# A gated MLP with adapters and an output projection in fp32 precision: the down projection's ten full blocks in seven block products instead of eight

## What is computed

```
x: (8 sequences, 256 tokens, H = 1024); F = 2752; adapters of rank 16, chosen per sequence
gate = x @ W_gate.T + 0.5 * (x @ A_gate.T) @ B_gate.T
up   = x @ W_up.T   + 0.5 * (x @ A_up.T)   @ B_up.T
act  = silu(gate) * up
x1   = x + act @ W_down.T + 0.5 * (act @ A_down.T) @ B_down.T
out  = x1 + x1 @ weight.T + bias + scale * (x1 @ A.T) @ B.T
```

## Time and profile before

| | us |
|---|---|
| median of three runs | 1662.97 |
| profiled execution, its own time | 1659.71 |
| its span | 1657.6 |
| PE busy | 1620.2 (98%) |
| DVE busy | 1138.4 (69%) |
| POOL busy | 653.5 (39%) |
| ACT busy | 500.8 (30%) |
| granted PE clock, mean | 0.996 |

### The profile page before, as it was taken

One profiled execution on the slowest core, in us unless ns is written; L12 is line 12 of the kernel. 1 busy time (PEld: TensorE's weight loads), 2 busy tenths in 40 slices (PEclk: granted clock), 3 DMA queues, 4 the chain that ended last, 5 costly groups with the idle time before them and its releaser, 6 DMA issues.

```text
span 1657.6 us, 20957 instructions
## 1 busy us (share of the span) xinstructions
PE 1620.2 (98%) x7060; PEld 1315.6 (79%) x7060; DVE 1138.4 (69%) x1302; ACT 500.8 (30%) x833; POOL 653.5 (39%) x441
## 2 busy tenths in 40 slices
PE   6989999999999899999999999999999999999998
PEld 4778888888887788888888788888888887778886
DVE  5987777777769877777777655666655578856433
ACT  3633333333346333333334221111111121431110
POOL 5244444444453444454444443233323331541110
PEclk9999999999999999999999999999999999999999
DMA  8334434433533345334334751122222131013322
GB/s 160 101 80 106 151 98 105 144 84 87 131 90 101 80 108 153 92 105 143 87 85 131 249 148 58 51 79 80 80 53 78 61 70 27 19 29 79 79 50 54
DMA packets 218125, 156.12 MB, mean 94 GB/s; under 512 B 110692, under 2 KB 200164, under 8 KB 215268
## 3 DMA queue, kind: packets, MB, share of 16 engines
q1 hardware_dynamic: 169536, 114.92, 27.4%
q10 hardware_dynamic: 48356, 39.86, 7.6%
q0 software_dynamic: 128, 0.00, 0.0%
HBM read 115.38 MB, written 39.32 MB: 93 GB/s over the span
## 4 chain that ended last, share of the span: by engine, by line
PE 64%; DVE 2%; POOL 1%; issue 1%; DMA 0%; ACT 0%; SPq 0%; DVEq 0%; ACTq 0%
PE ps L1958 64%; DVE tw_down L958 0%; POOL act L1884 0%; POOL Wd L1892 0%; DVE acc L950 0%; DVE X_T L608 0%; DMA raw<-in_x_dram 0%; POOL W L1843 0%; DVE Bd L904 0%; ACT W L1397 0%; DVE Bf L641 0%; DVE tw_down L933 0%; DVE tw_down L931 0%; DVE TU L508 0%; DVE ct L1077 0%
## 5 line engine op out<-in xcount | busy, mean ns | idle before, releaser
L1958 PE MATMUL ps<-X_T,W 128*128 128x512 f32 x1944 | 463.9, 393 | 13.0 <-DVE vbuf L688 5.1
L1958 PE MATMUL ps<-act,Wd 128*128 128x512 f32 x2016 | 462.2, 389 | 1.3 <-POOL Wd L1892 1.3
L1958 PEld LDWEIGHTS ps<-X_T,W 128*128 128x128 f32 x1944 | 365.9, 189 | 97.4 <-DVE vbuf L673 7.4
L1958 PEld LDWEIGHTS ps<-act,Wd 128*128 128x128 f32 x2016 | 378.4, 188 | 81.4 <-POOL Wd L1892 1.7
L1958 PE MATMUL ps<-X_B,W 128*128 128x512 f32 x1728 | 419.0, 392 | 15.3 <-ACT X_B L1426 12.8
L1958 PEld LDWEIGHTS ps<-X_B,W 128*128 128x128 f32 x1728 | 326.4, 189 | 86.6 <-issue 13.2
L950 DVE TENSOR_TENSOR acc<-acc,ps 128x1024 f32<-128x1024 f32 x176 | 214.1, 1219 | 176.5 <-PE ps L1958 175.8
L1843 POOL TENSOR_TENSOR W<-s,W 128x512 fp32r<-128x512 f32 x156 | 211.6, 1357 | 260.4 <-ACT W L1397 260.4
L1843 POOL TENSOR_TENSOR W<-TG,W 128x512 fp32r<-128x512 f32 x88 | 128.4, 1460 | 179.3 <-ACT W L1397 179.3
L1397 ACT ACTIVATE W<-s 128x512 fp32r<-128x512 f32 x156 | 98.4, 632 | 275.5 <-PE ps L1958 264.4
L1884 POOL TENSOR_TENSOR act<-stage,act 128x1024 fp32r<-128x1024 f32 x42 | 100.7, 2415 | 173.4 <-ACT act L1630 173.4
(11 more groups left out here) (135 smaller groups left out, 1522.7 us busy)
## 6 DMA issues: line engine op xcount, KB each, us to landing
stage<-act_scratch SPq DMA_DIRECT2D x21, 1024.0 KB, 5.0
raw<-in_L_cond_W_gate_dram SPq DMA_DIRECT2D x164, 128.0 KB, 3.0
raw<-in_L_cond_W_up_dram SPq DMA_DIRECT2D x164, 128.0 KB, 3.2
raw<-in_x_dram SPq DMA_DIRECT2D x104, 128.0 KB, 3.1
raw<-in_L_cond_W_down_dram SPq DMA_DIRECT2D x88, 128.0 KB, 3.3
act_scratch<-c21buf ACTq DMA_DIRECT2D x42, 256.0 KB, 2.4
act_scratch<-vbuf ACTq DMA_DIRECT2D x42, 256.0 KB, 2.8
xt_scratch<-xt ACTq DMA_DIRECT2D x4, 2048.0 KB, 6.6
```

What stands on the lines that cost most here:

```text
L1958: return nc.tensor.matmul(dst, stationary, moving, start=start, stop=stop, skip_group_check=True)
```

## The change

The full blocks are done in two groups of five. The 2x2 split is over the feature tile (2bb or 2bb+1) and the 512-token column on one side, and over feature tile and even or odd k on the other. In each group seven products (in the order P4, P2, P1, P5, P6, P3, P7) are formed for each token half h: 28 stages. A stage sums over the five blocks, one **step** per block, so there are 140 steps of four 128-row outputs p by THREE, 12 matmuls each. In P2, P1, P3 and P7 a step has two more matmuls, for the adapter. Each p has a bank; bank numbers rotate through seven, and the eighth is the adapter's.

- Phase A makes the sums of `act` that the products need (T1 to T4): four more two-input DVE instructions per two units (`t_first`, `t_second`, `t_fourth`), stored by ACT into `sums_scratch`. vbuf becomes two buffers.
- SP loads one [128, 512] moving operand per step (two in P7) through a ring of four `st`; ACT makes its high part in a ring of four `Tr`, POOL or DVE the low part. `mv_step` says at which step label each engine does it.
- Weights are turned into eight buffers `DW` (two transposes for each item), summed there in place by DVE (`down_sum`), and split into five `Sr`.
- DVE adds each bank to one to four places of `acc`, [128, 512] at a time (`read_bank`), and x from HBM at steps 40 to 87 (`add_residual`).
- `AD_STEP` says at which step label DVE turns the adapter weights of a block. A "label" q is the place in an engine's own order that `down_step(q)` fills.
- The Td and Bd chain stands after all steps.

```diff
+GROUP = 5
+T_RING = 4
+STAGING = 4
...
+        PRODUCTS = ["P4", "P2", "P1", "P5", "P6", "P3", "P7"]
+        B_USES = {"P4": "T4", "P2": "B21", "P1": "B11", "P5": "T1", "P6": "T2", "P3": "B22", "P7": "T3"}
+        B_GIVES = {"P1": ("C11", "C12", "C21", "C22"), "P2": ("C11",), "P3": ("C12",), "P4": ("C21",),
+                   "P5": ("C12", "C22"), "P6": ("C12", "C21", "C22"), "P7": ("C21", "C22")}
+
+        T_OF = {"P2": ("B21", 1, 0), "P1": ("B11", 0, 0), "P3": ("B22", 1, 1), "P7": ("B12", 0, 1)}
+        B_STAGES = [(g, name, h) for g in range(2) for name in PRODUCTS for h in range(2)]
+        STEPS = GROUP * len(B_STAGES)
...
+        def raw_at_step(q):
+
+            items = []
+            if 40 <= q < 88 and q % 3 == 1:
+                items.append(("r", (q - 40) // 24, (q - 40) // 3 % 8))
+            if q in (-1, 0, 1):
+                items += [("D", q + 3, 0), ("D", q + 3, 1)]
+            if 22 <= q < 34 and q % 2 == 0:
+                items.append(("D", 5 + (q - 22) // 4, (q - 22) // 2 % 2))
+            if 61 <= q < 65:
+                items.append(("D", 8 + (q - 61) // 2, (q - 61) % 2))
+            if q in (90, 92):
+                items.append(("D", BLOCKS - 1, (q - 90) // 2))
+            if q in (96, 98):
+                items.append(("Bd", (q - 96) // 2))
+            return items
+
...
+        AD_STEP = {1: 3, 2: 5, 3: 7, 4: 9, 5: 68, 6: 70, 7: 72, 8: 74, 9: 76, 10: 100}
...
+        def mv_step(n):
+
+            return MOVING[n - T_RING][0] + 1 if n >= T_RING else n - 3
+
+        def mv_by_vector(n):
+            q, name, _, h = MOVING[n]
+            return name == "B12" or (h == 1 and name != "T3")
+
...
+        def banks_at_step(q):
+            s, j = divmod(q, GROUP)
+            return s - 1, {0: (0, 1), 1: (2,), 2: (3,)}.get(j, ()) if s > 0 else ()
...
+        def bank_of(s, p):
+            return (4 * s + p) % 7
...
+                    eng.wait_ge(t_stored[1], 16 * (n - 1))
...
+                eng.wait_ge(t_stored[0], 16 * n)
...
+
...
+                V.tensor_tensor(c21buf[:, :], c21buf[:, :], t1buf[:, :], ALU.subtract).then_inc(t_made[3], 1)
...
+            def turn_down(bb, e):
+
+                src = take(("D", bb, e))
...
+                for c in range(2):
+                    last = V.transpose(
+                        DW[bb % len(DW)][:, c, :, e * 64:(e + 1) * 64].rearrange("p k (q i) -> p q k i", q=2),
+                        src[:, :].rearrange("p (q k c i) -> p c q k i", q=2, k=KT, c=2)[:, c])
+                last.then_inc(dw_turned.up((bb, e)), 1)
...
+            def read_bank(s, p):
+
+                eng.wait_ge(pe_s.sem, pe_s.after(("bank", s, p)))
+                for place in places_of(s, p):
+                    h, k, c = place
+                    dst, src = acc[h][:, k, c * TT:(c + 1) * TT], bank_b(bank_of(s, p))
+                    if place in written:
+                        eng.wait_ge(acc_added.sem, acc_added.after(written[place]))
+                        V.tensor_tensor(dst, dst, src, ALU.add).then_inc(acc_added.up((s, p, place)), 1)
+                    else:
+                        V.tensor_copy(dst, src).then_inc(acc_added.up((s, p, place)), 1)
...
+            def down_step(q):
+                s, banks = banks_at_step(q) if q >= 0 else (0, ())
+                for p in banks:
+                    read_bank(s, p)
+                    if p == 0 and s in T_STAGES:
+                        read_t_bank(s)
+                for item in raw_at_step(q):
+                    if item[0] == "r":
+                        add_residual(item)
+                for n in range(len(MOVING)):
+                    if mv_step(n) == q and mv_by_vector(n):
+                        moving_low(n)
+                if 0 <= q < STEPS and B_STAGES[q // GROUP][2] == 0:
+                    g, name, _ = B_STAGES[q // GROUP]
+                    at_ = still_at[g, name, g * GROUP + q % GROUP] + GROUP
+                    if at_ < len(STILL) and STILL[at_] in sw_sum.value:
+                        down_sum(STILL[at_])
+                for item in raw_at_step(q):
+                    if item[0] == "D" and item[1] < BLOCKS - 1:
+                        turn_down(*item[1:])
+                    elif item[0] != "r":
+                        turn_item(item)
+                for bb in range(1, BLOCKS):
+                    if AD_STEP[bb] == q:
+                        turn_ad(bb)
+                if q in (STEPS - 3, STEPS - 2):
+                    last_low(q - STEPS + 3)
...
+            for q in range(-3, STEPS + 3):
+                down_step(q)
+            for pr in range(2):
+                td_first(pr)
+            for p in range(2):
+                bd_low(p)
+            for p in range(2, 4):
+                turn_item(("Bd", p))
...
                 else:
                     sp.wait_ge(ad_turned, bb)
...
+            def load_moving(n):
+
+                _, name, j, h = MOVING[n]
+                if n >= STAGING:
+                    wait_mv_low(sp, n - STAGING)
...
+            def down_step(q):
+                for n, moving in enumerate(MOVING):
+                    if moving[0] == q + 6:
+                        load_moving(n)
+                for item in raw_at_step(q + 4):
+                    if item[0] == "D":
+                        load_down(item)
+                    elif item[0] == "Bd":
+                        load_bd(item)
+                    else:
+                        load_residual(item)
+                for bb in range(1, BLOCKS):
+                    if AD_STEP[bb] == q + 4:
+                        load_ad(bb)
...
+            def moving_high(n):
+                eng.wait_ge(mv_loaded[n % STAGING], 16 * (n // STAGING + 1))
+                if n >= T_RING:
+                    wait_step(eng, MOVING[n - T_RING][0])
+                else:
...
+            def down_step(q):
+                for n in range(len(MOVING)):
+                    if mv_step(n) == q:
+                        moving_high(n)
+                for n in {-3: (0, 1), -1: (2,), 0: (3,), 1: (4,)}.get(q, ()):
+                    still_high(STILL[n])
+                if still_for(q - 1) is not None:
+                    still_high(still_for(q - 1))
+                for bb in range(1, BLOCKS):
+                    if q == (AD_STEP[bb] + 1 if bb < BLOCKS - 1 else STEPS - 3):
+                        ad_high(bb)
...
+                wait_step(eng, STEPS - 1)
...
+            def down_step(q):
+                s, j = divmod(q, GROUP)
+                g, name, h = B_STAGES[s]
+                block_ = g * GROUP + j
+                n = mv_at[q, B_USES[name]]
+                slot, moving = Sr[j], Tr[n % T_RING]
+                eng.wait_ge(sw_lo, still_at[g, name, block_] + 1)
+                wait_mv_low(eng, n)
+                for p in range(4):
+                    if j == 0 and before_in_bank[s, p] is not None:
+                        wait_bank_read(eng, *before_in_bank[s, p])
...
+                    for wl, xl in THREE:
+                        last = matmul(bank_b(bank_of(s, p)), slot[:, wl, p, :], moving[:, xl, :],
+                                      start=(j == 0 and (wl, xl) == (0, 0)),
+                                      stop=(j == GROUP - 1 and (wl, xl) == (1, 0)))
```

734 lines of the change are left out of this document (449 added, 285 removed).

## The result

The changed kernel took **1730.22 us** (median of 4 runs, 1726.67 to 1731.03), against 1662.18 (4 runs): ratio **1.0405, 95% interval 1.0387 to 1.0423**, 68 us slower. I had forecast 1695 with a range of 1648 to 1724. The sign was right, the size was half, and the measured time lies 6 us above the range. The profiled execution took 1731.03 with a span of 1729.3, 71.7 more than the 1657.6 of before; all that follows divides these 71.7 us.

The account below looks back on a forecast made before the run. Phase B was taken as bound by PE's count of matmuls; -54.4 + 8 + 11 + 22 + 19 + 9 + 10.6 + 7 = +32 us on 1659.7 gave 1692, 1695 for the median, range 1648 to 1724.

Parts of the forecast that it names:

- Matmuls: Phase B's full blocks: 1680 matmuls in place of 1920, 240 x 0.227 us saved, -54.4 us.
- A_down's turns, first group: Labels 3 to 9: turns with their loads at least 9.3 us apart, but placed 5.4 apart; +22 us.
- Second group: A_down's turns at labels 68 to 76, with additions of x between: +19 us, at the least 13.
- Start of phase B: Steps 0 to 4: step 0 starts 6.2 us late, later weight items wait for loads; +11, bounds 8 to 14.
- Last block: After the last step PE waits 11.8 us for DVE's chain to Td; +10.6, bounds 8 to 13.
- Phase A: New DVE sums cost 0.8 us each in each half's first units, hidden in ordinary units; +8, bounds 0 to 18.
- ordinary units full: Sign expected in the trace: windows of phase A's ordinary units stay full as before, not beyond 20.06 us.
- DVE over the rest: Other phase B stages: DVE's bank reads and turns overfill some, late by 2.8 and 4.0; +9, bounds 3 to 20.
- 2 for the crowded P7 stages: P7's share of the +9 us for DVE in the rest of phase B: 2 us.
- Rival 3: P7: moving operands late through the ring of four, 20 steps lose 11 us; total 1725, chance 0.17.
- The clock: PE's clock falls after long waits, 1.4 us each, five of some ten holes counted; +7, bounds 2 to 15.
- Where the next wait ends late anyway it costs nothing: Phase B's holes: a lowered PE clock adds no time if the next wait ends late anyway.

Follow-up runs that it names:

- g5: Changed kernel with A_down turns spread, one transpose per A_down block, W_down earlier, activations in pieces, x and Bd work moved, `t_fourth` behind `add_v`: 1668.39 us, ratio 1.0041.
- j1: g5 with the eight DMAs of each A_down block issued four at a time at two labels, and x's additions at other labels: 1653.98 us, ratio 0.9963.
- g3: Changed kernel with PE multiplying zeros while it would wait, at twelve waits of phase B: 1728.46 us, ratio 1.0398.

## Why the prediction was right in sign and wrong in size

- **Matmuls.** Right: 1680, -52.0 for -54.4 us.
- **A_down's turns, first group.** Right in mechanism (turns 9.4 to 12.1 us apart; PE's waits of 2.18, 1.74, 4.80, 5.92 where the walk through the queues had 3.8, 1.3 with 2.6, 5.4 and about 10): 20.3 for 22. **Second group** 24.1 for 19, turns 10.8 to 12.5 apart.
- **Start of phase B.** 14.5 for 11: step 0 starts 6.0 late as computed, the other items of W_down come 3 us later than walked.
- **Last block.** PE waited 10.9 us for Td, forecast 11.8; 12.0 for 10.6.
- **Phase A: mis-sized.** "I take 0.8 each: +8" was 16.6 (12.1 to 16.9 in the ten traces). The ten sums of the first units took 10.9 us, 1.09 each, because four of them began behind a POOL instruction; these units lost 11.4 (16.6 less the next item). The ordinary ones, "hidden" by the prediction, had waits of 5.2: `t_fourth` stood directly ahead of `add_v`, which PE waits for, and the 3 us of DVE's idle time that the prediction counted on lies at another place of the unit. The promised sign "ordinary units full" failed by this much. With `t_fourth` behind `add_v` (g5) two of the nine waits are left. The rule of the Trainium skill (SBUF — State Buffer, "SBUF: two separate sides") says that a DVE instruction with two SBUF inputs and a GpSimd one shut each other out; the trace agrees in every one of the ten sums that met one: a sum that began second ended 0.55 us after the GpSimd instruction, and where that came second it ended 1.15 us after the sum. By that rule alone the prediction had 12.5 for the first units, nearer to their 11.4 than its own 8; over all 80 sums the means are only 0.67 to 0.85 us, as 70 met no GpSimd instruction.
- **"DVE over the rest", the step that failed.** It allowed "2 for the crowded P7 stages", and they lost 16.6. It counted DVE's work and left out SP's queue, where x's, W_down's and A_down's loads stand between the operands: without them P7 is late by 0.4 (g5). Rival 3 named P7, had 11 for it and at 1725 came nearest to the measured time, but its reason (a ring of four operands is short) isn't the cause: in g5 and j1 the same ring runs steps 60 to 69 without waits. Steps 11 to 59 and 80 to 134 lost 9.7 together, where the term had 2.8 and 4.0.
- **Left out, by the same step.** The 1.5 MB of the last block's activations, in the queue ahead of operands: 10.0 us. The prediction priced the last block's chain and not its loads, though it had walked A_down's loads through the same queue.
- **The clock.** Booked at +7 as a term of its own. g3 gives about 1 us for phase B, with its interval of 5: most of it lies inside waits that something else ends. "Where the next wait ends late anyway it costs nothing" was the right sentence, and for phase B's holes together it held. What the three more slow groups of phase A's first units cost is inside phase A's 16.6 and was not measured by itself. The Trainium skill (TensorE: Matmul & The Clock Gate, "HAM oscillation") tells of a price after every wait; the trace shows the slow matmuls, and g3 that in phase B they cost little or no time.

Against the +32 forecast 40 us are missing: +17 in P7 and the rest of DVE's term, +10 the activations, +9 phase A, +10 over the start, the second group and the last block, +2 matmuls, -2 first group, -7 the clock.

What stays open: how much of the start's 14.5 us is SP's issue of W_down (4 DMAs, 2.0 us per item) and how much the landing: no run separates them. Nor is it shown how the 11.4 us of the halves' first units are shared between DVE's sums and the slow matmuls behind PE's waits, or what A_down's loads alone cost P7.

## What to carry to other kernels

- A faster algorithm in the bound engine moves work to others; price the queue that feeds it (here SP with its waits) as carefully as the engines: walk each DMA in order, with issue time, landing, and the buffer that it waits for, and look where a long issue or a large transfer stands ahead of a small urgent one. Splitting it won 5 us in j1's steps 5 to 10, for no change in work.
- A hole that is due to several loads in one queue doesn't close when one is moved, and the whole time may hardly show the gain: x away and W_down earlier gave 2 and 5 us, within or near the noise, while the stretch itself was 7 us less late each time. Read such an edit by its stretch, and with A_down's loads moved too the hole was gone.
- Don't add the half clock to waits without asking what sets the next start: if another chain does, it costs nothing.
- An engine with idle time isn't free to take work over: ask which buffers wait for it. The four sums cost 41 us more on POOL than on DVE.

## What the runs showed of the hardware

- A transfer of 256 KB issued 2.2 us behind 1.5 MB in the same queue was used 10.7 us after its issue, against about 3 elsewhere, as if the queue moved its transfers in order (whether it does, no run shows by itself); four pieces with operands between them gave 5 us back. The Trainium skill (DMA: Bandwidth & Descriptors, "Two DMAs through the same engine are not ordered") says that what one queue has on an engine starts in order, though it may end out of it; the trace fits that.
- Eight DMAs of 64 pieces of 256 bytes took SP 5.75 us to issue, eight of 16 pieces of 1 KB 3.85.
- Sixteen transposes of 32x64 took 3.98 us, one of 128x256 that moves the same elements 0.44.
- A two-input DVE sum of 128x512 that began while POOL ran took 1.62 to 1.78 us and ended 0.55 us after POOL's instruction (five of five); alone, or begun first, it took 0.65 to 0.69, and the POOL instruction that came second ended 1.15 to 1.16 us after it (five of five; POOL's 1.29 became up to 1.59).
- Matmuls on zeros kept the granted clock up (0.98 for 0.94 over phase B's steps).
